# The next head's row of maxima goes into the free columns of the output bank

## The chip, the cores and the metric

The kernel runs on one core of a Trainium2 chip. The metric is device time in microseconds, the median over runs of the same compiled program.

## The reference

A block of three parts on 4 sequences of 1024 tokens of width 128: a mixture-of-experts layer at half weight, attention, and the same expert layer again. Cut to what matters here:

```python
x = x + 0.5 * ffn(layernorm(x))               # 8 experts, 2 chosen for each token
q, k, v = heads(layernorm(x) @ qkv_w + qkv_b)  # 16 heads of width 8, rotary q and k
scores  = einsum('bhqd,bhkd->bhqk', q, k) * 8 ** -0.5
attn    = softmax(scores) @ v                  # 4 x 16 = 64 pairs (b, h), each 1024 x 1024
x = x + attn @ out_w + out_b
x = x + 0.5 * ffn(layernorm(x))
```

The change touches only the attention part, the 64 pairs of sequence and head, called heads 0 to 63 below.

## The kernel before

Each engine has its own instruction stream, written out by hand and kept in step by semaphores. The attention loop handles a head in 16 half steps i = 0 to 15; two of them make one block kb = i // 2 of 128 keys. Four heads make one round of a hardware loop (`Fori`); 14 rounds (heads 4 to 59) run in the loop, the first and the last four heads are written out apart.

**What TensorE does.** In half step i of head n it issues `key_scores` (line 999): 128 keys by 512 queries, transposed scores into one PSUM bank. Beside it, in the other half of the array's rows, it issues `max_scores` (line 966) for head n+2: 128 queries by 512 keys, which serve only to find each query's maximum. After every odd i comes `weigh_values` (line 1014), which multiplies the exponentials of an earlier block (kb - 2) with the values and adds into the head's output bank. Only columns 0 to 255 of the 512 of that bank are used (`QW` = 256). The profile counts each of its four matmuls as two records, x8.

**What the others do.** VectorE reduces each pair of `max_scores` banks, 128 x 1024, to a maximum (line 1262, eight for a head); there are two such pairs of banks, taken in turn, and `max_scores` waits on `max_read` until the pair is free. ScalarE turns each score bank into exponentials (line 750, `probs`, 16 for a head), and copies the finished output of the head before out of PSUM after exponential 3 (line 738, `ot`). GpSimd splits the negated maxima into three bf16 parts (`mparts`).

**The row.** A head's maxima are needed as a row that is part of its query operand. Ahead of `key_scores` of i = 10 (`MT_AT`) of head n, TensorE transposes `mparts` of head n+1 into PSUM (`max_transpose`, line 988). ScalarE copies the result, 24 x 128, to `mrow` (line 730), between exponentials 9 and 10 in its own stream, and a DMA brings it into the operand Q for the next head.

**The ring of banks.** `key_scores` uses three banks in turn. The class `Banks` works out who uses which, and `bank_free` makes a matmul wait until the last user of its bank has been read. The row takes one place in this ring:

```python
if i == MT_AT:
    self.row_user[u] = self.back(user.get(ring[0]), n)
    self.row[u] = ring[0]
    user[ring[0]] = ("row", n, 0)
    ring.append(ring.pop(0))
```

So around the row, before: the transpose waits for exponential 7, key scores 10 for exponential 8, key scores 11 for exponential 9, and key scores 12 for the row's copy. Elsewhere key scores i wait for exponential i - 3 (after the swap of the output bank at i = 6, key scores 6 wait for the copy `ot`). The order of all this is fixed in the code; nothing is planned at run time.

Of the kernel before, what the change touches and what calls it, by code (L numbers as in the profile page):

```python
# [23 lines left out]
BF16 = mybir.dt.bfloat16  # L24
# [4 lines left out]
ACT = mybir.ActivationFunctionType  # L29
AX_X = mybir.AxisListType.X  # L30

P = 128
# [14 lines left out]
NH = B * H  # L47
KB = T // P
PARTS = 3
# [8 lines left out]
QW = T // QUARTERS  # L58
VW = 32
PIECE = H * CH // P  # L60
QSLOTS = 4
# [5 lines left out]
MT_AT = 10  # L67
# [19 lines left out]
class Banks:  # L87


    def __init__(self):  # L90
        self.key, self.row, self.out = ([{} for _ in range(QSLOTS)] for _ in range(3))
        self.key_user, self.row_user, self.out_user = ([{} for _ in range(QSLOTS)] for _ in range(3))
        ring, out = list(SCORE_BANKS), OUT_BANK
        user = {}
        for n in range(2 * QSLOTS):
            u = n % QSLOTS
            for i in range(HALVES):
                if i == OUT_AT:
                    self.out_user[u] = self.back(user.get(ring[0]), n)
                    ring[0], out = out, ring[0]  # L100
                    user[ring[0]] = ("out", n - 1, 0)
                    self.out[u] = out
                if i == MT_AT:
                    self.row_user[u] = self.back(user.get(ring[0]), n)
                    self.row[u] = ring[0]
                    user[ring[0]] = ("row", n, 0)
                    ring.append(ring.pop(0))
                self.key_user[u][i] = self.back(user.get(ring[0]), n)
                self.key[u][i] = ring[0]
                user[ring[0]] = ("key", n, i)  # L110
                ring.append(ring.pop(0))
            if u == QSLOTS - 1:
                assert tuple(ring) == SCORE_BANKS and out == OUT_BANK, (ring, out)
# [6 lines left out]
BANKS = Banks()  # L120
# [35 lines left out]
def build(nc, x_in, qkv_w, qkv_b, v_b, out_w, out_b, wr_t, w1_in, w2_t, cos_t, sin_t, out):  # L156
# [4 lines left out]
    with ExitStack() as ctx:  # L161
# [24 lines left out]
        identb = sb("identb", [P, P], BF16)  # L186
# [49 lines left out]
        mparts = sb("mparts", [P, 2, PARTS, KB], BF16)  # L236
        mrow = sb("mrow", [PARTS * KB, 2, P], BF16)
# [20 lines left out]
        score = [[ps[:, BANKS.key[u][i], :] for i in range(HALVES)] for u in range(QSLOTS)]  # L258
        maxps = [ps[:, MAX_BANK + 2 * s:MAX_BANK + 2 * s + 2, :] for s in range(2)]
        first_maxps = [ps[:, 2 * s:2 * s + 2, :] for s in range(FIRST_PAIRS)]  # L260
        mpsum = [ps[0:PARTS * KB, BANKS.row[u], 0:P // 2].bitcast(BF16) for u in range(QSLOTS)]
        opsum = [ps[:, BANKS.out[u], 0:QW] for u in range(QSLOTS)]


# [49 lines left out]
        mT_in_psum = sem("mT_in_psum")  # L314
# [301 lines left out]
        def _(sc):  # L616
# [106 lines left out]
            def mrow_copy(r, u, beside):  # L723
                n = QSLOTS * r + u
                sc.wait_ge(mT_in_psum, n + 1)

                if not (isinstance(r, int) and r == 0 and u < 2):
                    back = (u - 2) % QSLOTS
                    sc.wait_ge(mrow_loaded[back], 16 * (r + (1 if u >= 2 else 0)))
                nc.scalar.activation(mrow[:, u % 2, :], mpsum[beside], ACT.Copy).then_inc(mrow_ready, 1)  # L730

            def o_copy(r, u):
                n = QSLOTS * r + u
# [26 lines left out]
                    if i == 5 and not more:  # L760
                        xT_copy(NCH, 0, early_t)

            mrow_copy(0, 0, 0)
            for u in range(QSLOTS):
                head(0, u, first=(u == 0))
            with sc.Fori(1, NH // QSLOTS - 1) as r:
# [11 lines left out]
        def _(pe):  # L778
# [192 lines left out]
            def bank_free(n, last):  # L971


                what, dn, i = last
                if what == "key":
                    at_least(pe, probs_ready, HALVES * (n + dn) + i + 1)
                elif what == "row":
                    pe.wait_ge(mrow_ready, n + dn + 2)
                else:
                    at_least(pe, ot_ready, n + dn + 1)  # L980

            def max_transpose(r, u, beside, first=False):

                n = QSLOTS * r + u
                pe.wait_ge(mparts_ready, n + 1)
                if not first:
                    bank_free(n - 1, BANKS.row_user[beside])
                nc.tensor.transpose(mpsum[beside], mparts[:, u % 2, :, :].rearrange("p i t -> p (i t)"),
                                    identb[:]).then_inc(mT_in_psum, 1)

            def key_scores(r, u, i, row):

                n = QSLOTS * r + u
                kb, j = i // 2, i % 2
                if i == 0:
                    pe.wait_ge(mrow_loaded[u], 16 * (r + 1))
                last = BANKS.key_user[u][i]
                bank_free(n, BANKS.row_user[u] if last == ("row", 0, 0) and not row else last)
                nc.tensor.matmul(score[u][i], K[u][0:ROWS, kb * P:(kb + 1) * P],  # L999
                                 Q[u][0:ROWS, j * CH:(j + 1) * CH], start=True, stop=True).then_inc(scores_in_psum, 1)  # L1000

# [19 lines left out]
            pe.wait_ge(head_loaded[1], 32)  # L1021
            for i in range(HALVES):
                if i == FIRST_MT_AT:
                    max_transpose(0, 0, 0, first=True)
                max_scores(0, 1, i)

            pe.wait_ge(v_ready, NCH)
# [2 lines left out]
            def head(r, u, maxes=True, row=True, first=False, early=None, ahead=True):  # L1030
                for i in range(HALVES):
                    kb, j = i // 2, i % 2
                    if i == HALVES - 1 and ahead:
                        operands(r + (u + 3) // QSLOTS, (u + 3) % QSLOTS)
                    if i == MT_AT and row:
                        max_transpose(r + (u + 1) // QSLOTS, (u + 1) % QSLOTS, u)
                    key_scores(r, u, i, row)
                    if maxes:
                        max_scores(r + (u + 2) // QSLOTS, (u + 2) % QSLOTS, i)
                    if j == 1 and kb >= LAG:  # L1040
                        weigh_values(r, u, kb - LAG)
                    elif j == 1 and not first:
                        weigh_values(r + (u - 1) // QSLOTS, (u - 1) % QSLOTS, KB + kb - LAG)
                    if early == 0 and i == 5:

                        pe.wait_ge(max_read, KB * NH)
                        out_projection(0, early_t)
                    if early == 1 and i == 3:
                        x_transposes(NCH, 0, 0, early_t)
                    if early == 1 and i == 9:  # L1050
                        router(NCH, 0, 0, early_r)
# [11 lines left out]
            pe.wait_ge(mrow_ready, NH)  # L1063
            pe.wait_ge(gap_ready, NCH + 1)

            ffn(NCH, True)
# [377 lines left out]
```

## Time and profile before

| | |
|---|---|
| median of 3 runs | 1257.05 us (1257.0 to 1258.89) |
| profiled execution, time | 1257.09 us |
| profiled execution, span | 1255.3 us |
| busy: TensorE, VectorE, ScalarE, GpSimd | 1230.6, 1109.6, 802.1, 149.0 us |
| attention, from the first key scores to the last exponentials | 360 to 955 us |

Busy time is the time in which at least one instruction of the engine is shown as running; instructions overlap, so it says little about slack. The start times of single instructions say more: where the same instruction comes back at a fixed interval with nothing between, the interval is the engine's pace.

### The profile page before, as it was taken

The page shows a single profiled execution, that of the slowest core. Times are in us where ns is not written, and L with a number is a line of the kernel's source. Part 1 is how long each engine was busy: PE and PEld are TensorE (multiplying, and loading weights), DVE is VectorE, ACT ScalarE, POOL GpSimd, SP SyncE. Part 2 cuts the span into 40 slices and gives each one's busy share as a digit, 9 for nine tenths or more (in the row PEclk, how much of TensorE's full clock was granted, in tenths as well). Part 3 has the DMA queues.
Part 4 walks back from the last instruction along what each step waited for, and adds up shares of the span by engine and source line. Part 5 has one row for each costly group of instructions (what it writes and reads, how often), then busy time and mean ns, then how long its engine had stood idle before and what let it go on. Part 6 is the DMA issues. An engine that isn't in the chain of part 4 may idle for free.

```text
span 1255.3 us, 31378 instructions
## 1 busy us (share of the span) xinstructions
PE 1230.6 (98%) x10208; PEld 609.7 (49%) x10208; DVE 1109.6 (88%) x2256; ACT 802.1 (64%) x1546; POOL 149.0 (12%) x454
## 2 busy tenths in 40 slices
PE   6999999999899999999999999999999999999998
PEld 4776666676422222222222222222225777777776
DVE  7889888898789999999999999999995777787775
ACT  5533333333259999999999999999996333333332
POOL 0021222210241111111111111111110000000000
PEclk9999999999869999999999999999999999999999
DMA  7000111002102111111111111111111000000000
GB/s 214 1 26 28 49 51 49 26 29 70 51 21 80 34 42 32 38 36 32 42 32 42 32 32 42 32 42 32 36 47 42 16 18 28 28 28 27 10 9 9
DMA packets 54202, 48.43 MB, mean 39 GB/s; under 512 B 11632, under 2 KB 46960, under 8 KB 54128
## 3 DMA queue, kind: packets, MB, share of 16 engines
q1 hardware_dynamic: 54128, 47.48, 12.4%
q8 instruction: 41, 0.67, 0.2%
q14 instruction: 33, 0.27, 0.1%
HBM read 23.73 MB, written 23.33 MB: 37 GB/s over the span
## 4 chain that ended last, share of the span: by engine, by line
PE 96%; DVE 2%; ACT 1%; issue 0%; DMA 0%; DVEq 0%; ACTq 0%
PE ps L859 26%; PE ps L1014 23%; PE ps L999 22%; PE ps L846 18%; PE ps L814 1%; PE ps L836 1%; PE ps L781 1%; PE ps L966 1%; PE ps L823 1%; PE ps L853 1%; DVE mx L1262 1%; PE ps L873 0%; DVE X L1208 0%; ACT probs L750 0%; DMA X<-x_in 0%
## 5 line engine op out<-in xcount | busy, mean ns | idle before, releaser
L1262 DVE TENSOR_REDUCE mx<-ps 128x1 f32<-128x1024 f32 x512 | 586.0, 1216 | 9.3 <-PE ps L873 4.0
L750 ACT ACTIVATE probs<-ps 128x512 f32<-128x512 f32 x1024 | 551.2, 600 | 32.2 <-PE ps L999 27.7
L669 ACT ACTIVATE sg<-ps,unscale 128x512 f32<-128x512 f32 x256 | 173.6, 687 | 273.9 <-PE ps L859 273.5
L1014 PE MATMUL ps<-probs,vh 128*32 128x256 f32 x4096 | 328.2, 392 | 0.0
L999 PE MATMUL ps<-Q,K 51*128 51x512 bf16 x1024 | 321.6, 384 | 1.8 <-ACT probs L750 0.4
L966 PE MATMUL ps<-K,Q 48*128 48x512 bf16 x1008 | 319.5, 388 | 1.2 <-DVE mx L1262 0.6
L846 PEld LDWEIGHTS ps<-w,act 128*128 128x128 f32 x2048 | 247.9, 192 | 17.8 <-issue 0.8
L846 PE MATMUL ps<-w,act 128*128 128x128 f32 x2048 | 249.3, 275 | 0.0
L1196 DVE SCALAR_TENSOR_TENSOR act<-ps,unscale,sg 128x512 f32<-128x512 f32 x256 | 183.3, 746 | 42.7 <-PE ps L859 17.4
L859 PE MATMUL ps<-x_hi,w_hi 128*128 128x512 f16 x512 | 194.8, 381 | 1.7 <-DVE w_lo L1154 1.0
L859 PE MATMUL ps<-x_lo,w_hi 128*128 128x512 f16 x512 | 194.6, 380 | 0.0
L859 PE MATMUL ps<-x_hi,w_lo 128*128 128x512 f16 x512 | 194.5, 380 | 0.0
L1208 DVE SCALAR_TENSOR_TENSOR X<-ps,rw,X 128x128 f32<-128x128 f32 x512 | 143.9, 344 | 53.8 <-PE ps L846 52.3
L999 PEld LDWEIGHTS ps<-Q,K 51*128 51x128 bf16 x1024 | 75.6, 93 | 227.0 <-ACT probs L750 160.1
L1014 PEld LDWEIGHTS ps<-probs,vh 128*32 128x32 f32 x4096 | 80.9, 108 | 187.6 <-ACT probs L750 146.8
L859 PEld LDWEIGHTS ps<-x_hi,w_lo 128*128 128x128 f16 x512 | 50.2, 98 | 60.9 <-issue 0.8
L966 PEld LDWEIGHTS ps<-K,Q 48*128 48x128 bf16 x1008 | 74.8, 93 | 9.1 <-DVE mx L1262 8.3
L859 PEld LDWEIGHTS ps<-x_hi,w_hi 128*128 128x128 f16 x512 | 51.7, 101 | 53.3 <-issue 3.8
L859 PEld LDWEIGHTS ps<-x_lo,w_hi 128*128 128x128 f16 x512 | 50.2, 98 | 49.8 <-issue 4.9
L559 POOL TENSOR_SCALAR negm<-mx 128x8 f32<-128x8 f32 x64 | 15.1, 236 | 455.6 <-DVE mx L1262 455.6
L517 POOL TENSOR_TENSOR qf<-rot 128x512 f32<-128x512 f32 x14 | 17.8, 1273 | 233.4 <-DVE rot L1243 233.4
L659 ACT ACTIVATE tanh_gap<-gap 128x4 f32<-128x4 f32 x16 | 3.3, 207 | 54.7 <-DVE gap L1165 54.7
(89 smaller groups left out, 605.2 us busy)
## 6 DMA issues: line engine op xcount, KB each, us to landing
o_parts<-ot SPq DMA_DIRECT2D x64, 128.0 KB, 1.9
q_stack<-parts SPq DMA_DIRECT2D x96, 64.0 KB, 2.0
k_stack<-parts SPq DMA_DIRECT2D x96, 64.0 KB, 2.0
Q<-q_stack SPq DMA_DIRECT2D x64, 96.0 KB, 2.3
K<-k_stack SPq DMA_DIRECT2D x64, 96.0 KB, 2.3
probs<-w_in SPq DMA_DIRECT2D x8, 256.0 KB, 5.1
att<-o_parts SPq DMA_DIRECT2D x16, 128.0 KB, 2.6
rden<-rdens SPq DMA_DIRECT2D x16, 128.0 KB, 2.6
```

Of the source, the lines that this page charges most:

```text
L517: nc.gpsimd.tensor_tensor(qf[:, w, :], rot[:, w, 0, :], rot[:, w, 1, :], ALU.add).then_inc(rot_sum, 1)
L559: seq.then(nc.gpsimd.tensor_scalar(negm[:, 0, :], mx[:, s, :], -1.0, None, ALU.mult))
L669: nc.scalar.activation(sg[:, j, :], hid[2 * j], ACT.Silu, scale=unscale[:, e, 2 + j:3 + j]).then_inc(silu_done, 1)
L750: nc.scalar.activation(probs[:, kb % PSLOTS, j * CH:(j + 1) * CH], score[u][i], ACT.Exp, scale=SCALE).then_inc(probs_ready, 1)
L846: last = nc.tensor.matmul(ypsum[s][:, t, :], act[:, s, j, t * P:(t + 1) * P], w2[:, e, j, :], start=(j == 0), stop=(j == 1))
L859: last = nc.tensor.matmul(bank, w[:, e, at:at + P], x[:, k, :], start=(n == 0), stop=(n == 2))
L966: last = nc.tensor.matmul(maxps[t % 2][:, half, :], Q[u][0:STACK, t * P:(t + 1) * P], K[u][0:STACK, half * CH:(half + 1) * CH], start=True ...
L999: nc.tensor.matmul(score[u][i], K[u][0:ROWS, kb * P:(kb + 1) * P], Q[u][0:ROWS, j * CH:(j + 1) * CH], start=True, stop=True).then_inc(scor ...
L1014: last = nc.tensor.matmul(opsum[u][VW * c:VW * (c + 1), :], vh[:, u % 2, kb, :], probs[:, kb % PSLOTS, c * QW:(c + 1) * QW], start=(kb == ...
L1196: nc.vector.scalar_tensor_tensor(out=act[:, e % 2, j, :], in0=hid[2 * j + 1], scalar=unscale[:, e, j:j + 1], in1=sg[:, j, :], op0=ALU.mult ...
L1208: last = nc.vector.scalar_tensor_tensor(out=xt, in0=ypsum[e % 2][:, t, :], scalar=rw[:, k, t, e:e + 1], in1=xt, op0=ALU.mult, op1=ALU.add)
L1262: nc.vector.tensor_reduce(mx[:, u % 2, t:t + 1], pair.rearrange("p a b -> p (a b)"), AX_X, ALU.max).then_inc(max_read, 1)
```

## The change

The transposed row no longer has a place in the ring. It is written into columns 256 to 383 of the output bank of the head that is being worked on, beside the sums that `weigh_values` builds there. Since that bank holds a sum in the making, the row is written by an ordinary matmul with the identity, with `start=False`, and it arrives as fp32, where a transpose left bf16. And since ScalarE must not read a bank that TensorE writes, TensorE now waits for the row's copy (`mrow_ready`) ahead of the next `weigh_values`, behind key scores and max scores 11. The first head's row, ahead of the loop, is transposed as before, into bank 1. ScalarE copies from the new place.

```diff
-                if i == MT_AT:
-                    self.row_user[u] = self.back(user.get(ring[0]), n)
-                    self.row[u] = ring[0]
-                    user[ring[0]] = ("row", n, 0)
-                    ring.append(ring.pop(0))
...
-        mpsum = [ps[0:PARTS * KB, BANKS.row[u], 0:P // 2].bitcast(BF16) for u in range(QSLOTS)]
+        mpsum = [ps[0:PARTS * KB, BANKS.out[u], QW:QW + P] for u in range(QSLOTS)]
+        first_mpsum = ps[0:PARTS * KB, 1, 0:P // 2].bitcast(BF16)
...
-            def max_transpose(r, u, beside, first=False):
+            def max_transpose(r, u, beside):
                 n = QSLOTS * r + u
                 pe.wait_ge(mparts_ready, n + 1)
-                if not first:
-                    bank_free(n - 1, BANKS.row_user[beside])
-                nc.tensor.transpose(mpsum[beside], mparts[:, u % 2, :, :].rearrange("p i t -> p (i t)"),
-                                    identb[:]).then_inc(mT_in_psum, 1)
+                rows = mparts[:, u % 2, :, :].rearrange("p i t -> p (i t)")
+                if beside is None:
+                    nc.tensor.transpose(first_mpsum, rows, identb[:]).then_inc(mT_in_psum, 1)
+                else:
+                    nc.tensor.matmul(mpsum[beside], rows, identb[:], start=False, stop=True, skip_group_check=True).then_inc(mT_in_psum, 1)
...
                     if maxes:
                         max_scores(r + (u + 2) // QSLOTS, (u + 2) % QSLOTS, i)
+                    if i == MT_AT + 1 and row:
+                        pe.wait_ge(mrow_ready, QSLOTS * r + u + 2)
                     if j == 1 and kb >= LAG:
                         weigh_values(r, u, kb - LAG)
```

TensorE's stream in the loop around the row, in a head of the first place of a round, before: from the weighing ahead of the row to key scores 12.

```order
L1014 MATMUL ps<-probs,vh 32x256 x3
L84 REGISTER_ALU [waits mparts_ready]
L988 MATMUL ps<-identb,mparts 24x128 [waits probs_ready]
L84 REGISTER_ALU
L999 MATMUL ps<-Q,K 128x512 [waits probs_ready]
L965 REGISTER_ALU
L966 MATMUL ps<-K,Q 128x512 [waits max_read]
L84 REGISTER_ALU
L999 MATMUL ps<-Q,K 128x512 [waits probs_ready]
L966 MATMUL ps<-K,Q 128x512
L1014 MATMUL ps<-probs,vh 32x256 [waits probs_ready]
L999 MATMUL ps<-Q,K 128x512 [waits mrow_ready]
```

The same place in the changed kernel (line 985 is the row, 994 the key scores, 962 the max scores, 1009 the weighing):

```order
L1009 MATMUL ps<-probs,vh 32x256 x3
L985 MATMUL ps<-identb,mparts 24x128 [waits mparts_ready]
L84 REGISTER_ALU
L994 MATMUL ps<-Q,K 128x512 [waits probs_ready]
L961 REGISTER_ALU
L962 MATMUL ps<-K,Q 128x512 [waits max_read]
L84 REGISTER_ALU
L994 MATMUL ps<-Q,K 128x512 [waits probs_ready]
L962 MATMUL ps<-K,Q 128x512
L1009 MATMUL ps<-probs,vh 32x256 [waits probs_ready,mrow_ready]
L84 REGISTER_ALU
L994 MATMUL ps<-Q,K 128x512 [waits probs_ready]
```

The row has lost its wait for an exponential, the wait for the row's copy has moved from key scores 12 up to the weighing in front of them, and the waits of key scores 10, 11 and 12 are now for exponentials 7, 8 and 9, one earlier than before for the first two. ScalarE's stream has the same instructions in the same order as before; here its piece around the row in the changed kernel, for the second place of a round (line 746 are the exponentials, 726 is the row's copy):

```order
L84 REGISTER_ALU [waits scores_in_psum]
L746 ACTIVATE probs<-ps 128x512 [waits probs_used]
L742 REGISTER_ALU
L746 ACTIVATE probs<-ps 128x512 [waits scores_in_psum]
L721 REGISTER_ALU
L725 REGISTER_ALU [waits mT_in_psum]
L726 ACTIVATE mrow<-ps 24x128 [waits mrow_loaded3]
L742 REGISTER_ALU
L84 REGISTER_ALU [waits scores_in_psum]
L746 ACTIVATE probs<-ps 128x512 [waits probs_used]
```

The row's copy still stands behind exponentials 8 and 9 and ahead of exponential 10.

## Rows read from the trace of the kernel before

**Rows 1.** The page: TensorE's busy time, and the chain that ended last by engine.

```profile
PE 1230.6 (98%) x10208; PEld 609.7 (49%) x10208; DVE 1109.6 (88%) x2256; ACT 802.1 (64%) x1546; POOL 149.0 (12%) x454
...
PE 96%; DVE 2%; ACT 1%; issue 0%; DMA 0%; DVEq 0%; ACTq 0%
```

**Rows 2.** One round of four heads: stretch, its length, busy time by engine, clock.

```profile
451.75:488.52 36.77, 36.68 (x392) 10.65 (x388) 36.58 (x33) 35.33 (x73) 5.01 (x24) 1.00 0.12 36
```

**Rows 3.** Timeline of TensorE around a row: start, length, what.

```profile
707.56 0.64 PE L1014 MATMUL ps<-probs,vh 128*32 128x256 f32 x8
708.13 0.39 PE L999 MATMUL ps<-Q,K 51*128 51x512 bf16 x1
...
708.36 0.38 PE L999 MATMUL ps<-Q,K 51*128 51x512 bf16 x1
...
708.66 0.64 PE L1014 MATMUL ps<-probs,vh 128*32 128x256 f32 x8
709.12 0.22 PE L988 MATMUL ps<-identb,mparts 128*24 128x128 bf16 x1
709.28 0.39 PE L999 MATMUL ps<-Q,K 51*128 51x512 bf16 x1
...
709.77 0.39 PE L999 MATMUL ps<-Q,K 51*128 51x512 bf16 x1
...
710.09 0.64 PE L1014 MATMUL ps<-probs,vh 128*32 128x256 f32 x8
710.66 0.39 PE L999 MATMUL ps<-Q,K 51*128 51x512 bf16 x1
```

**Rows 4.** Timeline of ScalarE there: exponentials 7 and 8, 8, 9, the copy.

```profile
708.02 1.21 ACT L750 ACTIVATE probs<-ps 128x512 f32<-128x512 f32 x2
...
708.63 0.60 ACT L750 ACTIVATE probs<-ps 128x512 f32<-128x512 f32 x1
...
709.12 0.59 ACT L750 ACTIVATE probs<-ps 128x512 f32<-128x512 f32 x1
709.60 0.25 ACT L730 ACTIVATE mrow<-ps 24x128 bf16<-24x128 bf16 x1
```

**Rows 5.** Timeline of VectorE in several stretches: start, length of a merged run, count.

```profile
705.59 1.22 DVE L1262 TENSOR_REDUCE mx<-ps 128x1 f32<-128x1024 f32 x1
...
705.59 4.61 DVE L1262 TENSOR_REDUCE mx<-ps 128x1 f32<-128x1024 f32 x4
...
708.98 2.47 DVE L1262 TENSOR_REDUCE mx<-ps 128x1 f32<-128x1024 f32 x2
...
699.74 2.55 DVE L1262 TENSOR_REDUCE mx<-ps 128x1 f32<-128x1024 f32 x2
...
924.18 10.27 DVE L1262 TENSOR_REDUCE mx<-ps 128x1 f32<-128x1024 f32 x9
```

**Rows 6.** The row's transposes from 441 to 893 us: durations, first and last start.

```profile
L988 PE MATMUL ps<-identb,mparts x50: 219/219/219, 442.6 to 893.0; 128*24 128x128 bf16 x50
```

**Rows 7.** ScalarE's two kinds of copies: shortest, median, longest ns, first and last start.

```profile
L730 ACT ACTIVATE mrow<-ps x64: 252/253/267, 353.5 to 940.4; 24x128 bf16<-24x128 bf16 x64
L738 ACT ACTIVATE ot<-ps x64: 384/390/427, 375.6 to 955.9; 128x256 f32<-128x256 f32 x64
```

**Rows 8.** Timeline at a row whose copy found ScalarE idle.

```profile
369.02 0.31 PE L988 MATMUL ps<-identb,mparts 128*24 128x128 bf16 x1
...
369.37 0.27 ACT L730 ACTIVATE mrow<-ps 24x128 bf16<-24x128 bf16 x1 [0.44 <-PE ps L988]
```

**Rows 9.** Timeline of TensorE at a row ahead of the hardware loop.

```profile
387.55 0.22 PE L988 MATMUL ps<-identb,mparts 128*24 128x128 bf16 x1
...
388.44 0.42 PE L1014 MATMUL ps<-probs,vh 128*32 128x256 f32 x4
```

**Rows 10.** The last max scores on TensorE; all maxima, with the last start.

```profile
932.65 0.38 PE L966 MATMUL ps<-K,Q 48*128 48x512 bf16 x1
...
L1262 DVE TENSOR_REDUCE mx<-ps x512: 1160/1215/1226, 329.2 to 933.2; 128x1 f32<-128x1024 f32 x171
```

More of the change, by code:

```diff
@@ L90, in __init__ @@
     def __init__(self):
-        self.key, self.row, self.out = ([{} for _ in range(QSLOTS)] for _ in range(3))
-        self.key_user, self.row_user, self.out_user = ([{} for _ in range(QSLOTS)] for _ in range(3))
+        self.key, self.out = ([{} for _ in range(QSLOTS)] for _ in range(2))
+        self.key_user, self.out_user = ([{} for _ in range(QSLOTS)] for _ in range(2))
         ring, out = list(SCORE_BANKS), OUT_BANK
@@ L729, in mrow_copy @@
                     sc.wait_ge(mrow_loaded[back], 16 * (r + (1 if u >= 2 else 0)))
-                nc.scalar.activation(mrow[:, u % 2, :], mpsum[beside], ACT.Copy).then_inc(mrow_ready, 1)
+                nc.scalar.activation(mrow[:, u % 2, :], first_mpsum if beside is None else mpsum[beside], ACT.Copy).then_inc(mrow_ready, 1)
             def o_copy(r, u):
@@ L761, in head @@
                         xT_copy(NCH, 0, early_t)
-            mrow_copy(0, 0, 0)
+            mrow_copy(0, 0, None)
             for u in range(QSLOTS):
@@ L976, in bank_free, with key_scores @@
                     at_least(pe, probs_ready, HALVES * (n + dn) + i + 1)
-                elif what == "row":
-                    pe.wait_ge(mrow_ready, n + dn + 2)
                 else:
                     at_least(pe, ot_ready, n + dn + 1)
-            def max_transpose(r, u, beside, first=False):
+            def max_transpose(r, u, beside):
                 n = QSLOTS * r + u
                 pe.wait_ge(mparts_ready, n + 1)
-                if not first:
-                    bank_free(n - 1, BANKS.row_user[beside])
-                nc.tensor.transpose(mpsum[beside], mparts[:, u % 2, :, :].rearrange("p i t -> p (i t)"),
-                                    identb[:]).then_inc(mT_in_psum, 1)
-            def key_scores(r, u, i, row):
+                rows = mparts[:, u % 2, :, :].rearrange("p i t -> p (i t)")
[3 more added lines that the diff above has]
+                    nc.tensor.matmul(mpsum[beside], rows, identb[:], start=False, stop=True, skip_group_check=True).then_inc(mT_in_psum, 1)
+            def key_scores(r, u, i):
                 n = QSLOTS * r + u
@@ L996, in key_scores @@
                     pe.wait_ge(mrow_loaded[u], 16 * (r + 1))
-                last = BANKS.key_user[u][i]
-                bank_free(n, BANKS.row_user[u] if last == ("row", 0, 0) and not row else last)
+                bank_free(n, BANKS.key_user[u][i])
                 nc.tensor.matmul(score[u][i], K[u][0:ROWS, kb * P:(kb + 1) * P],
@@ L1023, in _ @@
                 if i == FIRST_MT_AT:
-                    max_transpose(0, 0, 0, first=True)
+                    max_transpose(0, 0, None)
                 max_scores(0, 1, i)
@@ L1036, in head @@
                         max_transpose(r + (u + 1) // QSLOTS, (u + 1) % QSLOTS, u)
-                    key_scores(r, u, i, row)
+                    key_scores(r, u, i)
                     if maxes:
                         max_scores(r + (u + 2) // QSLOTS, (u + 2) % QSLOTS, i)
+                    if i == MT_AT + 1 and row:
+                        pe.wait_ge(mrow_ready, QSLOTS * r + u + 2)
                     if j == 1 and kb >= LAG:
@@ L1062, in _ @@
             pe.wait_ge(ot_ready, NH)
-            pe.wait_ge(mrow_ready, NH)
             pe.wait_ge(gap_ready, NCH + 1)
```

## Prediction

> **What bounds the kernel now.** I read the page first. The chain that ended last is TensorE in 96%, and TensorE is busy 98% of the span [rows 1]. That doesn't tell what a change in attention is worth, since VectorE is nearly as full there: in one round of four heads, 36.77 us long, TensorE is busy for 36.68 us, VectorE for 36.58 and ScalarE for 35.33, at full clock [rows 2]. Three engines look saturated, so shares decide nothing, and I went to start times.
>
> TensorE's timeline shows the weighings (line 1014) at 707.56 and 708.66, 1.107 us apart in finer figures, and the next at 710.09, 1.43 later [rows 3]. So seven blocks of a head take TensorE 1.107 us each, and the block with the row takes 1.427: 7 x 1.107 + 1.427 = 9.176 us a head. The extra 0.32 us isn't the transpose itself. Key scores 10 start 0.16 after the transpose, but key scores 11 come 0.49 after those [rows 3], where two neighbours elsewhere in a head are 0.23 apart (708.13 and 708.36). ScalarE's rows say why: exponential 9 starts at 709.12 and lasts 0.59, so it ends at 709.71, and key scores 11 start 0.06 later [rows 3, 4]. Exponential 8 ends at 709.23, and key scores 10 start 0.05 behind it. The ring has lost a bank to the row, so TensorE waits for two exponentials that elsewhere it wouldn't need.
>
> VectorE follows. One maximum shows 1.22 us, four in a row 4.61, so they start (4.61 - 1.22) / 3 = 1.13 us apart [rows 5]. The longest undisturbed run, nine in 10.27 us, gives 1.131 [rows 5]. This is VectorE's pace with nothing to wait for: 8 x 1.131 = 9.05 us a head. At the row two maxima take 2.47 instead of 2.35 us, and in the head that stands two places behind the start of a loop round 2.55 [rows 5]. So VectorE idles 0.12 us a head in three heads and 0.20 in the fourth, 0.14 on average. It agrees with the transposes: 50 of them between 442.6 and 893.0, so 49 heads of 9.19 us [rows 6]; 9.19 - 9.05 = 0.14.
>
> TensorE sets the pace by 0.14 us a head, and right below it lies VectorE's floor of 9.05 us. This is the figure that limits any gain here.
>
> **The change part by part.** *The ring place.* Key scores 10 and 11 now wait for exponentials 7 and 8, each one exponential (0.49 us, 708.63 to 709.12 [rows 4]) earlier. Both are done when TensorE comes there: key scores 10 may start 0.15 after the row, key scores 11 0.23 later, so 0.38 behind the row where now it is 0.65. By this alone the weighing could follow 0.31 later at 0.69, instead of 0.97 [rows 3].
>
> *The new wait.* The weighing must now wait for the row's copy. The copy stands behind exponential 9 on ScalarE and starts 0.48 behind the row (709.12 to 709.60 [rows 3, 4]); it lasts 0.25, and 0.06 is the delay from an end on ScalarE to a start on TensorE measured above. So the weighing starts 0.48 + 0.25 + 0.06 = 0.79 behind the row: 0.10 is idle time of a new kind, and of 0.28 won 0.18 is left. Behind the waiting instruction stand key scores 12 and max scores 12, so ScalarE and VectorE would both feel a longer wait; VectorE works on an earlier pair then. The block with the row becomes 0.46 (708.66 to 709.12) + 0.79 = 1.25 us, and TensorE's head 7 x 1.107 + 1.25 = 9.00, with the 0.02 that a loop round adds on average 9.02. That is below VectorE's 9.05, so VectorE becomes the bound, by a hair.
>
> *What the row costs.* The trace has no identity matmul of this shape that isn't a transpose. From below it is the 0.219 us of the transpose [rows 6], from above the 0.39 of a 512-column matmul [rows 3]; I take 0.22, since columns and operands are the same. At 0.39 key scores 11 and the weighing would come 0.17 later, at 0.86 behind the row, and the head would be 9.09: saving 0.10 instead of 0.14. The copy isn't hurt as much: with ScalarE idle it started 0.35 behind the row [rows 8], now it starts at 0.48 because exponential 9 is ahead of it. The Trainium skill's page "Perfetto Trace Analysis" says under "Transposes" that a logical transpose should use the transpose and not a standard matmul, which speaks against this part. By that rule the row gets dearer; the sum by it would be the 9.09 just given.
>
> *The copy.* It now reads fp32. From below it is 0.25 us as now, from above the 0.39 of the copy of 128 x 256 fp32 [rows 7]; I take 0.25, since there are still 128 elements a partition. At 0.39 the weighing starts at 0.93, the head is 9.16, and 0.03 a head is saved.
>
> *Nothing else.* The DMA that follows the copy has the rest of the head, over 6 us, and its place in the queue stays. The first head's row keeps its form. What is moved in the register work is a single instruction from in front of the row to behind the weighing, under its 0.57 us (710.09 to 710.66 [rows 3]).
>
> *The sum.* VectorE's idle time at the row goes away in the heads whose maxima lie beside loop heads 4 to 59: 56 x 0.14 = 7.9 us. The heads ahead of the loop have a shorter stall (the weighing 0.89 behind the row [rows 9], so 0.08 less, hence 0.04 above VectorE's floor instead of 0.12); three of them and the restart give 0.2. Head 62 has no maxima any more and TensorE runs alone, so its row saves the full 0.18. Last, a bound VectorE lets TensorE run ahead as far as the two pairs of banks allow: the pair's second matmul would start 2 x 1.131 - 1.22 - 0.06 - 0.23 = 0.76 ahead of its maximum, where the last one now starts 0.58 ahead (932.65 to 933.2 [rows 10]): 0.2 more for what follows. Together 7.9 + 0.2 + 0.2 + 0.2 = 8.5 us. The profiled execution took 1257.09 us, of it 1255.3 span, and is equal to the median of 1257.05: 1257.1 - 8.5 = 1248.6 us.
>
> **The rivals.** A measurement of this kernel can tell about 0.2%, 2.5 us, from no change.
>
> *TensorE stays the bound.* VectorE's floor is only 0.03 above TensorE's new pace, so anything that lengthens the wait for the copy by more is paid in full. For it: neither the fp32 copy nor the matmul is in the trace, and a restart behind a wait at the weighing isn't either. Against: both have the same element count. With the dear matmul the time is 56 x 0.10 + 0.4 = 6.0 less, 1251.1; with the dear copy 56 x 0.03 + 0.4 = 2.1 less, 1255.0.
>
> *No change.* The copy stands behind the same exponential 9 that holds key scores 11 now. If the wait for it cost 0.18 us more than I count (dear copy and a little more), one stall would have replaced the other: 1257.
>
> *Slower.* The new wait puts TensorE at the mercy of ScalarE's queue. If ScalarE reaches exponential 9 later, by more than the 0.18 us that is left, each further 0.1 costs 56 x 0.1 = 5.6 us, since VectorE and ScalarE both wait behind the weighing. The place is the backlog that the copy `ot` (0.39 us behind exponential 3 [rows 7]) makes: a backlog of 0.3 that still stood at exponential 8 would give 56 x 0.12 = 6.7 us more, 1263.8. Against: exponential 8 starts 0.61 behind exponential 7 (708.02 to 708.63), where full pace is 0.49, so ScalarE has caught up by then, with 0.12 to spare [rows 4], and blocks get no shorter. "Perfetto Trace Analysis" has under "Matmuls" the rule that independent matmul groups should rotate through different banks, so that evacuation overlaps the next group. The change goes against that, and by the rule the evacuation lies bare; what of it lies bare here by rows is the 0.10 us above.
>
> **How the numbers follow.** VectorE's floor, 1248.6: 0.74, its own range 1247.9 to 1249.7. TensorE still the bound, 1250 to 1255: 0.14. No change: 0.07. Slower: 0.05. The range from 1247.7 to 1253.0 holds the first and two thirds of the second, some 0.83. Of the second a small part lies within 0.2% of before, so faster 0.87, same 0.08, slower 0.05.
>
> **What would show it.** Maxima 1.131 us apart through the row, without the 2.47 and 2.55; the rows' matmuls 9.05 us apart in every head; key scores 11 about 0.4 behind the row and the weighing 0.6 to 0.8 behind it; `max_scores` waiting for VectorE in ordinary blocks, which TensorE's timeline doesn't show now. I am wrong if the weighing starts more than 0.85 behind the row, if the copy takes over 0.3 us, or if maxima slow down once they run without a pause.

## The result, and the profile after

The changed kernel takes 1248.37 us (median of 4 runs: 1250.74, 1247.19, 1249.06, 1247.67), the kernel before 1257.88 us in its 4 runs beside it (1257.0 to 1258.89). The ratio is 0.9929, with a 95% interval of 0.9917 to 0.9942: faster by 0.7%. Forecast were 1248.6 us, from 1247.7 to 1253.0. The profiled execution of the changed kernel is the slowest of its four, 1250.74 us, and that needs an explanation of its own, below. Two of its four times lie under the lower end of the range.

Line numbers of the changed kernel: the row is line 985, key scores 994, max scores 962, the weighing 1009, the row's copy 726, the exponentials 746, VectorE's maxima 1259.

The profile's page of the changed kernel, the lines that answer to [rows 1]: busy time by engine, then the chain that ended last by engine and by line.

```profile
PE 1224.7 (98%) x10208; PEld 617.9 (49%) x10208; DVE 1104.0 (88%) x2256; ACT 803.0 (64%) x1546; POOL 149.0 (12%) x454
...
PE 53%; DVE 35%; issue 10%; ACT 0%; DMA 0%; DVEq 0%; ACTq 0%
DVE mx L1259 34%; PE ps L855 27%; PE ps L842 18%; PE ps L1009 2%; PE ps L994 1%; PE ps L810 1%; PE ps L832 1%; PE ps L777 1%; PE ps L819 1%; PE ps L849 1%; PE ps L869 0%; PE ps L962 0%; DVE X L1205 0%; ACT probs L746 0%; PE ps L795 0%
```

Busy time tells as little as before: TensorE is still at 98%. The chain tells it: it was TensorE for 96%, and now VectorE's maxima hold 34% of it, and most of the 10% "issue" are the 0.2 to 0.3 us between one maximum and the next. In attention the bound has passed from TensorE to VectorE.

VectorE's timeline in the changed kernel: start, length of a run, count.

```profile
698.71 1.21 DVE L1259 TENSOR_REDUCE mx<-ps 128x1 f32<-128x1024 f32 x1
...
698.71 9.13 DVE L1259 TENSOR_REDUCE mx<-ps 128x1 f32<-128x1024 f32 x8
...
599.16 101.89 DVE L1259 TENSOR_REDUCE mx<-ps 128x1 f32<-128x1024 f32 x90
```

In the stretch up to 701 us ninety maxima run without a pause, eleven heads long: (101.89 - 1.21) / 89 = 1.131 us apart. The runs of [rows 5] with 2.47 and 2.55 us for two maxima are gone.

The rows' matmuls in the changed kernel, from 440 to 880 us (answers to [rows 6]), and the copies of the whole kernel (answers to [rows 7]): shortest, median and longest ns, first and last start.

```profile
L985 PE MATMUL ps<-identb,mparts x49: 219/219/219, 440.8 to 875.2; 128*24 128x128 bf16 x49
...
L726 ACT ACTIVATE mrow<-ps x64: 252/253/267, 353.2 to 931.3; 24x128 bf16<-24x128 f32 x63, 24x128 bf16<-24x128 bf16 x1
```

(875.2 - 440.8) / 48 = 9.05 us a head, where it was 9.19. The matmul with the identity takes 219 ns like the transpose before, and the copy out of fp32 253 ns like the copy out of bf16.

TensorE's timeline around a row in the changed kernel (answers to [rows 3]).

```profile
702.77 0.64 PE L1009 MATMUL ps<-probs,vh 128*32 128x256 f32 x8
703.23 0.22 PE L985 MATMUL ps<-identb,mparts 128*24 128x128 bf16 x1
703.38 0.39 PE L994 MATMUL ps<-Q,K 51*128 51x512 bf16 x1
...
703.60 0.38 PE L994 MATMUL ps<-Q,K 51*128 51x512 bf16 x1
...
703.99 0.64 PE L1009 MATMUL ps<-probs,vh 128*32 128x256 f32 x8
704.56 0.39 PE L994 MATMUL ps<-Q,K 51*128 51x512 bf16 x1
```

Key scores 11 start 0.38 behind the row, where it was 0.65, and the weighing 0.76, where it was 0.97. The block with the row takes 703.99 - 702.77 = 1.22 us instead of 1.43.

The same timeline at an ordinary block, and the same stretch of ScalarE with the row's copy (answers to [rows 4]).

```profile
699.95 0.39 PE L994 MATMUL ps<-Q,K 51*128 51x512 bf16 x1
699.98 0.39 PE L962 MATMUL ps<-K,Q 48*128 48x512 bf16 x1
```

```profile
703.68 0.25 ACT L726 ACTIVATE mrow<-ps 24x128 bf16<-24x128 f32 x1
```

In an ordinary block the max scores now start 0.03 behind the key scores: they wait for VectorE to give their banks back. (With shorter maxima, in e6 below, both start at 601.84 again.) At the row the two start together (703.38 both in the full timeline), since there TensorE is late and the banks are free. The copy starts 0.45 behind the row and ends at 703.93, 0.06 ahead of the weighing: what the weighing waits for is the copy.

**Where the 6.4 us of the span came from.** VectorE's last maximum starts at 924.3 instead of 933.2 [rows 10], 8.9 us earlier. Of these, 0.3 lie ahead of the first key scores, 0.7 in the heads ahead of the loop, 7.8 in the loop and 0.1 at its exit. After the last maximum 2.5 us are given back. These are the windows from the last maximum to the first matmul of the last expert layer, first of the changed kernel (with the stretch of 6.8 us inside it), then of the kernel before: stretch, length, busy time of TensorE, its weight loads, VectorE, ScalarE and GpSimd, then the granted clock, DMA share and GB/s.

```profile
924.30:949.90 25.60, 24.67 (x201) 7.77 (x197) 11.07 (x52) 19.64 (x42) 1.75 (x6) 0.87 0.04 12
930.00:940.00 10.00, 9.80 (x86) 2.67 (x86) 4.83 (x27) 9.55 (x20) 0.00 (x0) 1.00 0.05 15
942.00:948.80 6.80, 6.80 (x44) 1.73 (x47) 2.25 (x20) 3.35 (x7) 0.00 (x0) 0.50 0.00 0
```

```profile
933.30:956.30 23.00, 22.03 (x205) 7.30 (x197) 10.99 (x52) 19.78 (x42) 1.76 (x6) 1.00 0.04 13
```

In the changed kernel's profiled execution the granted clock falls to one half (1.2 GHz) from 942.0 to 948.8, in head 63. TensorE's timeline there shows two key scores in 1.03 us and a weighing of 1.08 us, where at full clock the weighing lasts 0.64:

```profile
943.11 1.08 PE L1009 MATMUL ps<-probs,vh 128*32 128x256 f32 x8
944.12 1.03 PE L994 MATMUL ps<-Q,K 51*128 51x512 bf16 x2
945.08 1.08 PE L1009 MATMUL ps<-probs,vh 128*32 128x256 f32 x8
```

Up to there TensorE was hardly idle: from 930 to 940 it was busy for 9.80 of 10 us. One gap follows, of 0.44 us, in which key scores wait for an exponential, and then the eight matmuls of the next expert layer's router, which have only 8 columns each. These stand in the changed kernel's timeline right ahead of the fall:

```profile
940.24 0.39 PE L994 MATMUL ps<-Q,K 51*128 51x512 bf16 x1 [0.44 <-ACT probs L746]
...
941.12 1.09 PE L832 MATMUL ps<-wr,xnT 128*128 128x8 f32 x8
```

The change added no work in heads 62 and 63. Whether this fall belongs to the change at all is asked by the runs from e8 on.

### The profile page after: what moved, and what is told of

The parts are those of the page before. It is cut to its first block, busy times and chain, and to the rows that moved or that the text cites. A ratio compares the mean times of both kernels' runs of the same rounds, so it can differ in the third digit from the quotient of the medians.

```text
span 1248.9 us, 31420 instructions
## 1 busy us (share of the span) xinstructions
PE 1224.7 (98%) x10208; PEld 617.9 (49%) x10208; DVE 1104.0 (88%) x2256; ACT 803.0 (64%) x1546; POOL 149.0 (12%) x454
## 4 chain that ended last, share of the span: by engine, by line
PE 53%; DVE 35%; issue 10%; ACT 0%; DMA 0%; DVEq 0%; ACTq 0%
DVE mx L1259 34%; PE ps L855 27%; PE ps L842 18%; PE ps L1009 2%; PE ps L994 1%; PE ps L810 1%; PE ps L832 1%; PE ps L777 1%; PE ps L819 1%; PE ps L849 1%; PE ps L869 0%; PE ps L962 0%; DVE X L1205 0%; ACT probs L746 0%; PE ps L795 0%
## 5 line engine op out<-in xcount | busy, mean ns | idle before, releaser
L994 PE MATMUL ps<-Q,K 51*128 51x512 bf16 x1024 | 312.1, 385 | 0.4 <-ACT probs L746 0.4
L962 PE MATMUL ps<-K,Q 48*128 48x512 bf16 x1008 | 309.0, 387 | 1.4 <-DVE mx L1259 0.6
L994 PEld LDWEIGHTS ps<-Q,K 51*128 51x128 bf16 x1024 | 83.2, 93 | 206.4 <-ACT probs L746 167.0
L962 PEld LDWEIGHTS ps<-K,Q 48*128 48x128 bf16 x1008 | 82.7, 93 | 9.4 <-DVE mx L1259 8.6
```

## The experiments

**My theory:** the gain is the ring place. Key scores 10 and 11 no longer wait for exponentials 8 and 9, TensorE's head falls below VectorE's floor of 9.05 us, and VectorE takes over. **The rivals:** the matmul with the identity or the new wait has a part in it, as a gain or a cost that another part hides; TensorE, not VectorE, is still the bound; and the wait for the copy can turn the gain into a loss if the copy comes more than 0.18 us later.

### The two other parts of the change alone

The wait alone, in the kernel before (e1_wait_only):

```diff
                         max_scores(r + (u + 2) // QSLOTS, (u + 2) % QSLOTS, i)
+                    if i == MT_AT + 1 and row:
+                        pe.wait_ge(mrow_ready, QSLOTS * r + u + 2)
                     if j == 1 and kb >= LAG:
```

> The kernel before, row still in the ring, with one thing added: TensorE also waits for the row's copy ahead of the weighing that follows key scores 11. Theory (the stall is the ring's wait for exponentials 8 and 9, and the new wait ends sooner than it): the copy's wait would end 0.79 us behind the row, the weighing starts 0.97 behind it anyway, so heads stay at 9.19 us on average and the time at 1257, within 1.5 us. Rival (the new wait costs TensorE something wherever it stands, as an extra instruction and a restart): 0.05 us or more a head, 1260 or more.

The matmul alone, into the ring bank that the transpose had (e2_matmul_in_ring):

```diff
-        mpsum = [ps[0:PARTS * KB, BANKS.row[u], 0:P // 2].bitcast(BF16) for u in range(QSLOTS)]
+        mpsum = [ps[0:PARTS * KB, BANKS.row[u], 0:P] for u in range(QSLOTS)]
...
-                nc.tensor.transpose(mpsum[beside], mparts[:, u % 2, :, :].rearrange("p i t -> p (i t)"),
-                                    identb[:]).then_inc(mT_in_psum, 1)
+                nc.tensor.matmul(mpsum[beside], mparts[:, u % 2, :, :].rearrange("p i t -> p (i t)"),
+                                 identb[:], start=True, stop=True).then_inc(mT_in_psum, 1)
```

> The kernel before with only the form of the row changed: a matmul with the identity into the ring bank in place of the transpose, fp32, copied from fp32. Theory: the form brings nothing and costs nothing; the row shows 0.22 us and the copy 0.25, the heads stay at 9.19, the time at 1257 within 1.5 us. Rival (part of the gain comes from the form): 1255 or less. Rival (an ordinary matmul is dearer than a transpose): key scores 10 move from 0.16 behind the row to up to 0.33; since exponential 9 holds key scores 11 the time may hide that, so the rows decide.

Measured: ratios to the kernel before of 1.0003 (0.999 to 1.0015) and 1.0003 (0.9993 to 1.0012). In both, the head stays at 9.192 us and the weighing 0.97 behind the row. These are the rows' matmuls and the copies of e2 over the whole kernel.

```profile
L988 PE MATMUL ps<-identb,mparts x64: 218/219/280, 352.9 to 938.8; 128*24 128x128 bf16 x64
...
L730 ACT ACTIVATE mrow<-ps x64: 254/254/266, 353.2 to 939.2; 24x128 bf16<-24x128 f32 x64
```

219 and 254 ns, against 219 and 253 of the bf16 forms [rows 6, 7]. Neither part brings or costs anything by itself, so what the whole change brings is the ring place (with the output bank as the place that makes it free). This is by elimination: no run frees the ring place alone, since the row must go somewhere. The wait alone costs nothing here because exponential 9 holds the same block for longer: in e1 the copy ends 0.24 us ahead of the weighing.

### The wait for the copy made longer

The changed kernel with one (e3_two_copies) or two (e4_three_copies) useless copies of the row ahead of the real one on ScalarE:

```diff
+                nc.scalar.activation(spare[:], first_mpsum if beside is None else mpsum[beside], ACT.Copy)
                 nc.scalar.activation(mrow[:, u % 2, :], first_mpsum if beside is None else mpsum[beside], ACT.Copy).then_inc(mrow_ready, 1)
```

> The changed kernel with a second, useless copy of the row ahead of the real one on ScalarE, which makes the copy end about 0.18 us later. Theory (TensorE's pace lies 0.03 to 0.04 us a head below VectorE's floor and the wait for the copy is on it): the weighing starts about 0.95 behind the row, the heads go from 9.05 to about 9.18, and the time rises by 57 x 0.13 = 7 us to about 1255. Rival (VectorE bounds and hides ScalarE's delay): under 2 us more, about 1249.

> The changed kernel with two useless copies of the row ahead of the real one. Theory: another 0.18 us on each head, all of it paid: heads of 9.36 us, some 17 to 18 us above the changed kernel, 1266, which is slower than the kernel before; this is the slower rival of the prediction made to happen. Rival (the delay is hidden behind VectorE): under 1252.

Measured against the kernel before: e3 0.9995 (0.9982 to 1.0008), e4 1.008 (1.006 to 1.01). Timelines of a row in e3 and in e4: start, length, what.

```profile
615.38 0.22 PE L987 MATMUL ps<-identb,mparts 128*24 128x128 bf16 x1
...
615.86 0.25 ACT L727 ACTIVATE spare<-ps 24x128 bf16<-24x128 f32 x1
616.02 0.26 ACT L728 ACTIVATE mrow<-ps 24x128 bf16<-24x128 f32 x1
...
616.33 0.42 PE L1011 MATMUL ps<-probs,vh 128*32 128x256 f32 x4 [0.19 <-ACT mrow L728]
```

```profile
610.95 0.22 PE L988 MATMUL ps<-identb,mparts 128*24 128x128 bf16 x1
...
611.74 0.26 ACT L729 ACTIVATE mrow<-ps 24x128 bf16<-24x128 f32 x1
...
612.06 0.62 PE L1012 MATMUL ps<-probs,vh 128*32 128x256 f32 x5 [0.35 <-ACT mrow L729]
```

The weighing now starts 0.95 and 1.11 behind the row, each time 0.06 behind the end of the real copy, and the heads take 9.168 and 9.328 us. Both are somewhat below what I had expected (9.18 and 9.36), since small copies stand 0.16 apart on ScalarE and not 0.18. With the weighing at 0.763 the head was 9.050: 0.18 more of wait cost 0.12, and the next 0.16 cost 0.16 in full. The kink is what two nearly equal bounds look like. So the wait for the copy is on TensorE's path, it has about 0.06 us of cover by VectorE, and the slower rival is real: at 0.34 us more it takes the whole gain and 0.8% with it.

The forecast time of e3, 1255 us, came in its profiled execution (1254.8) and three more of its ten (1254.82 to 1255.62); the other six lie from 1258.31 to 1259.63, so its median missed by 3.5 us. Its profile has no half clock at the end; the split of the times into groups comes up again below.

The Trainium skill's page "Perfetto Trace Analysis" asks under "Matmuls" that independent matmul groups rotate through different banks. In these runs what the breach of it costs follows how late the copy ends: in e3, e4 and e6 (below) TensorE's head is 8.22 us plus the distance of the weighing from the row, each time.

### How far TensorE lies below VectorE's floor

VectorE made faster in both kernels: its maxima read 768 of 1024 columns, with everything else as it is (e5_before_short_max, e6_after_short_max):

```diff
+SEEN = 3 * 2 * 512 // 4
...
-                nc.vector.tensor_reduce(mx[:, u % 2, t:t + 1], pair.rearrange("p a b -> p (a b)"), AX_X,
+                nc.vector.tensor_reduce(mx[:, u % 2, t:t + 1], pair.rearrange("p a b -> p (a b)")[:, 0:SEEN], AX_X,
```

> The kernel before, with VectorE's maxima over 768 of the 1024 columns of each pair (so the row of maxima leaves out a quarter of the keys). One maximum takes about 0.87 us in place of 1.13. Theory (TensorE set the pace before, through its stall at the row): the heads in the loop stay at 9.19 us; only the first two heads and the first eight maxima, which VectorE bounds, get shorter, by 2 to 5 us in all. Rival (VectorE was already a bound together with TensorE): the heads get shorter, toward 9.0 or less, and the time falls by 10 us or more.

> The changed kernel with the same shorter maxima (a quarter of the keys left out of the row). Theory: VectorE no longer bounds and TensorE's own pace shows: 9.00 us a head, 9.02 with the loop's share, so only 0.03 to 0.04 us a head less than the 9.05 of the changed kernel, about 2 us in all beside the 2 to 5 us of the start that the kernel before gains too. Rival (TensorE could have gone much faster): heads of 8.9 us or less, 8 us or more on top.

Measured against the kernel before: e5 0.9982 (0.9969 to 0.9995), e6 0.9902 (0.9877 to 0.9927). VectorE's timeline of e5:

```profile
598.72 0.96 DVE L1263 TENSOR_REDUCE mx<-ps 128x1 f32<-128x768 f32 x1
599.82 6.49 DVE L1263 TENSOR_REDUCE mx<-ps 128x1 f32<-128x768 f32 x6
606.78 0.96 DVE L1263 TENSOR_REDUCE mx<-ps 128x1 f32<-128x768 f32 x1 [0.47 <-PE ps L967]
```

A maximum lasts 0.96 instead of 1.22 us, but six of them stand (6.49 - 0.96) / 5 = 1.106 us apart, which is TensorE's pace, and at the row VectorE idles 0.47 us for the max scores. The heads of the loop stay at 9.19: a faster VectorE changes nothing there, so TensorE was the bound. Of the 0.2%, 1.1 us lie ahead of the loop, where the maxima of head 1 take 8.41 instead of 9.48 us. TensorE's timeline at a row in e6, from the block ahead of it:

```profile
601.84 0.38 PE L995 MATMUL ps<-Q,K 51*128 51x512 bf16 x1
601.84 0.38 PE L963 MATMUL ps<-K,Q 48*128 48x512 bf16 x1
602.14 0.64 PE L1010 MATMUL ps<-probs,vh 128*32 128x256 f32 x8
602.60 0.22 PE L986 MATMUL ps<-identb,mparts 128*24 128x128 bf16 x1
...
602.98 0.38 PE L995 MATMUL ps<-Q,K 51*128 51x512 bf16 x1
...
603.39 0.42 PE L1010 MATMUL ps<-probs,vh 128*32 128x256 f32 x4
```

With VectorE out of the way the weighing is 0.79 behind the row, the block with the row lasts 1.25 us, and the head takes 9.008. That is TensorE's own head in the changed kernel. It lies 0.04 below VectorE's 9.050: VectorE is the bound, by a hair. The weighing stands 0.41 behind the second key scores (603.39 - 602.98) where in the block before it is 0.30 (602.14 - 601.84): 0.11 us is what the wait for the copy costs TensorE. One of e6's times is 1243.21 us, the other three lie from 1247.32 to 1247.51, and the profiled one of these has the half clock at the end.

### No row at all

In the changed kernel, from head 4 on, neither matmul, copy nor DMA of the row (e7_no_row):

```diff
             def head(r, u, maxes=True, row=True, first=False, early=None, ahead=True):
+                row = row and isinstance(r, int) and r == 0 and u < 3
```

with the matching conditions at ScalarE's copy and SyncE's DMA, and key scores and GpSimd that no longer wait for it. The operands keep the rows of heads 0 to 3.

> The changed kernel with the row left out from head 4 on: no transpose, no copy, no DMA of the row, the operands keep the rows of heads 0 to 3. Theory: VectorE's floor holds the heads at 9.05 us, the same as with the row, though TensorE alone would need 8 x 1.107 = 8.86; the time is that of the changed kernel less at most 1 us (head 62 has no maxima to hold it). Rival (the row still costs something on the bound): up to 0.19 us a head less, 1240 or below.

Measured: 0.993 (0.9906 to 0.9954), 1248.86 us, the same as the changed kernel within the interval. VectorE's timeline of e7:

```profile
599.62 100.77 DVE L1261 TENSOR_REDUCE mx<-ps 128x1 f32<-128x1024 f32 x89
```

(100.77 - 1.21) / 88 = 1.131 us. Without the row the head is the same 9.05 us: the change has taken all that was to be had at this place, and what is left of the row costs nothing while VectorE is the bound.

### The fall of the clock at the end

The half clock of 6.8 us in head 63 stands in the profiles of e1, e2, e4, e5 and e6 as well, and not in those of the kernel before, e3 and e7. So it comes with and without the change. What sets heads 62 and 63 apart from the loop is that no max scores run beside the key scores: TensorE is busy by time, but the key scores use 51 of the 128 rows with nothing beside them. To test that, e8_after_filled_tail puts a useless matmul of the max scores' shape beside each key score there; e9_after_again is the changed kernel once more, e10_filled_tail_again is e8 once more.

```diff
+            def filler(u, i):
+                s, t, half = (u + 2) % QSLOTS, i // 2, i % 2
+                if u == 2 and i == 0:
+                    pe.wait_ge(max_read, KB * NH - 1)
+                nc.tensor.matmul(ps[:, MAX_BANK, :], Q[s][0:STACK, t * P:(t + 1) * P],
+                                 K[s][0:STACK, half * CH:(half + 1) * CH], start=True, stop=True)
...
                     if maxes:
                         max_scores(r + (u + 2) // QSLOTS, (u + 2) % QSLOTS, i)
+                    else:
+                        filler(u, i)
```

> The changed kernel with useless matmuls, shaped like max scores, beside each key score of heads 62 and 63, which have no max scores of their own, into a bank that is free there. In the profiled execution of the changed kernel TensorE's clock fell to half for 6.8 us from about 942 us, inside head 63, and the stretch from the last maximum to the first matmul of the last part took 25.6 us where the kernel before took 23.1. Theory (the clock falls there because TensorE does less in these two heads): the clock stays at full in that stretch, 22.7 to 23.1 us of it, and the runs come together near 1247.5 instead of 1247.2 to 1250.7. Rival (the fall has another cause, or depends on chance only): it still shows in some executions and the runs scatter as before.

> The changed kernel once more, beside the next three on one chip. The profiles so far show TensorE's clock at half for 27.3, 30.7 or 34.1 us from about 336 us, and for 6.8 us or not at all in head 63 (half in it in six of ten profiles); by rows these cost about 1.0 to 1.9 us and 2.9 us. Theory: with heads of 9.05 us in every execution, the time falls into groups between 1247 and 1251, median 1247.5 to 1250.

> The changed kernel with the useless matmuls in heads 62 and 63 once more. Theory (the fall in head 63 comes from too little work on TensorE there): no half clock in the profile between 900 and 1200 us, and no time in the highest group: all within 1247.0 to 1249.6. Rival (chance): the half clock shows again, or single times near 1251.

Measured: e8 0.9921 (0.9901 to 0.994), e9 0.993 (0.9915 to 0.9945), e10 0.9923 (0.991 to 0.9936). Windows from the last maximum to the first matmul of the last expert layer, for e8, e9 and e10:

```profile
925.80:948.60 22.80, 21.86 (x234) 7.32 (x230) 11.09 (x52) 19.68 (x42) 1.75 (x6) 1.00 0.04 13
```

```profile
925.40:950.80 25.40, 24.46 (x204) 7.72 (x197) 11.10 (x52) 19.69 (x42) 1.75 (x6) 0.87 0.04 12
```

```profile
924.60:947.40 22.80, 21.86 (x234) 7.35 (x231) 11.04 (x52) 19.69 (x41) 1.75 (x6) 1.00 0.04 13
```

With more matmuls (x234 instead of x204) the stretch is 2.6 us shorter, and the clock stays up. What e8 expected of the times, that they come together near 1247.5, didn't come: they lie from 1247.21 to 1249.38.

The filling isn't the only thing that sets the place apart. In each of the eight profiles with the fall, it comes 0.7 to 2.1 us behind the start of the router's eight matmuls in head 63. But the same gap and the same eight matmuls stand in all 14 profiles, and so in the ones where the clock stays up; here is e12, which has the filled tail:

```profile
940.06 0.39 PE L1001 MATMUL ps<-Q,K 51*128 51x512 bf16 x1 [0.43 <-ACT probs L746]
...
940.95 1.06 PE L832 MATMUL ps<-wr,xnT 128*128 128x8 f32 x8
```

No run moves or leaves out the router's matmuls, so their part in the fall isn't tested.

A second place where a half clock stands is the start of attention, from 336 us on for 27 to 34 us. e11_filled_start puts 12 useless matmuls beside the max scores of head 1, e12_filled_both has both fillings.

```diff
+                if i < HALVES - 4:
+                    nc.tensor.matmul(ps[:, 2, :], w1_hi[HALF:HALF + STACK, 0, 0:P], x_hi[HALF:HALF + STACK, 0, :],
+                                     start=True, stop=True)
                 max_scores(0, 1, i)
```

> The changed kernel with twelve useless matmuls beside the max scores of head 1 (about 351 to 358 us), in the other half of the rows, where TensorE otherwise waits for VectorE at half clock. Theory (the half clock of about 31 us from 336 us lasts as long as TensorE has little to do, and slows heads 0 and 1): it ends about 7 us earlier, the maxima of head 2, which took 11.2 to 12.5 us, take under 10.5, and the time falls by 1 to 3 us. Rival: the clock comes back at the same time as before, no gain.

> The changed kernel with both fillings, start and tail. Theory: the two gains add: no half clock in the tail, a shorter one at the start, times of 1244.5 to 1248 with less scatter, and the fastest of all versions by its median. Rival: no better than the better one of the two alone.

Measured: e11 0.9928 (0.9915 to 0.9941), e12 0.992 (0.9908 to 0.9933), 1247.64 us. Windows of e11 at the start:

```profile
335.50:352.60 17.10, 13.08 (x34) 4.90 (x34) 11.63 (x29) 5.33 (x8) 5.13 (x9) 0.50 0.02 8
352.60:356.00 3.40, 2.17 (x16) 0.52 (x14) 3.40 (x4) 1.55 (x2) 3.32 (x4) 1.00 0.13 35
356.00:369.70 13.70, 12.98 (x60) 2.31 (x56) 11.58 (x10) 6.75 (x14) 4.82 (x11) 0.50 0.03 7
```

In e11 the clock came back for 3.4 us only. In that stretch TensorE was busy for 2.17 of 3.40 us, and the clock fell again. The maxima of head 2 took 11.74 us, where under 10.5 were expected. The theory that this filling would end the slow stretch falls; it ends no sooner than without, and no time is gained. In e12, with the same filling, the clock didn't come back at all for 30.7 us from 337.0 on, though TensorE was busy for 3.32 of the 3.40 us from 352.6 to 356.0. So the short return can't be put down to the filling, and e12's median, which lies in the range expected of it, holds no gain at the start. The tail, again, has no half clock:

```profile
924.10:946.90 22.80, 21.86 (x234) 7.35 (x231) 11.05 (x52) 19.68 (x41) 1.75 (x6) 1.00 0.04 12
```

**What the times say with it.** The changed kernel with an unfilled tail (its own runs, e9 and e11, 16 times) has 7 times from 1250.39 to 1251.6, 8 from 1247.14 to 1247.67, and one at 1249.06. With the filled tail (e8, e10, e12, 14 times) none lies above 1249.4. The 3 profiles of the former have the half clock in head 63, the 3 of the latter don't. With a fall in 8 of 11 unfilled profiles, three without one could come by luck; 0 of 14 times against 7 of 16 say more (on the chip of e9 to e12, 0 of 10 against 6 of 12). The upper group disappears, but the medians, 1247.6 to 1248.9 against 1248.4 to 1249.4, aren't told apart by their intervals. The best version measured is e12 at 0.992, and it isn't shown to beat the plain change at 0.993. Nor is it shown what in the filling counts, the filled rows or just more matmuls.

## Why the prediction was right

- **What bounded the kernel before.** TensorE's 9.19 us above VectorE's floor of 9.05: e5 shows the first (a faster VectorE changes no head of the loop), e7 and the run of 90 maxima the second (9.05 with and without the row).
- **The ring place.** Key scores 11 were to start 0.38 behind the row, and start 0.378 behind it. That the gain is this part and no other follows from e1 and e2, where the other two do nothing alone.
- **The new wait.** The weighing at 0.79 behind the row by the sum; 0.763 measured, and 0.787 in e6. That it waits for the copy is shown by e3 and e4, which move it one for one. The waits on TensorE from 450 to 850 us put a number on the idle time of a new kind, below: engine, what it waited for, us in total, times, longest.

```profile
PEld ps L1009 <- ACT mrow L726: 19.9, 45, 0.5
```

  These 45 waits, 0.44 us each, are counted from the end of the last weight load and so hold more than matmul idle time; the loss to the path was put at 0.10 us (0.79 against 0.69), and e6's rows show 0.11. No run has the changed kernel without the wait, so 0.69 itself isn't measured.
- **The row's matmul and its copy.** 0.22 and 0.25 us forecast, 0.219 and 0.253 measured. Of the two bounds the lower one held for both. The rule of the Trainium skill's page "Perfetto Trace Analysis" under "Transposes", that a standard matmul should not stand in for the transpose, finds nothing to warn of in this shape: e2 exchanges one for the other at 219 ns each.
- **The block and TensorE's head.** 1.25 and 9.02 us forecast; 1.22 measured beside the bound VectorE, 1.25 and 9.01 in e6, where TensorE runs by its own pace.
- **The loop.** 56 x 0.14 = 7.9 us forecast, 7.8 measured, or 7.9 with the 0.1 at the exit. This is the main term, and its mechanism is the one that was forecast.
- **The small terms, mis-sized.** The heads ahead of the loop gave 0.7 instead of 0.2 us. Some 0.4 of it is head 2, whose maxima took 11.23 instead of 11.66 us in a stretch where the clock is half at first; in e8 the same head took 12.47, so this is scatter of the clock and no gain to count on. For the tail, its last row and TensorE's lead, 0.4 were forecast; at full clock it is 22.8 us (e8, e10, e12, though with the filling in it) against 23.0 to 23.1 before, which is 0.2 to 0.3. TensorE's lead for it was worked out as 0.76 us; the terms given add up to 0.75, which changes nothing.
- **What the sum didn't have, and luck.** The half clock in head 63 costs 2.6 to 3.0 us (25.4 to 25.6 us of tail against 22.8 in the changed kernel, 26.0 in e1 and e2 against 23.1 before) and came in 7 of 16 executions, by the times. It isn't part of the change: the kernel before scatters too, 24 of its 53 times on record lie from 1256.37 to 1257.39 us and the others from 1258.7 up. The sum started from an execution in the lower group (1257.09). The lower group of the changed kernel lies at 1247.14 to 1247.67, which is 9.7 us below that of the kernel before, by their medians, and under the forecast range; 8.5 were forecast. That the median of 1248.37 comes within 0.3 us of 1248.6 is luck: it lies between the two groups of times. The two profiles account for 9.2 us with the tail at full clock (8.9 and 0.3), of which 0.7 is scatter (0.3 ahead of attention, 0.4 in head 2); without that it is the forecast 8.5. What makes up the rest to 9.7 isn't known.

What stays open: why the clock falls in some executions and not in others with the same instructions, whether the router's matmuls in head 63 have a part in it, and what would keep it up at the start of attention.

## What to carry to other kernels

When several engines look full, take each one's pace in a head (the interval of its back-to-back instructions) and look for the block that breaks it: here one of eight blocks was 0.32 us too long, and the worth of any cure was capped at 0.14 by the next engine's floor. A buffer that is used once a head but takes a place in a ring costs the users behind it a step of slack, here key scores 10 and 11; columns that lie free in a bank with another rhythm cost none, provided that what empties them ends before the next writer needs the bank, and an extra copy in that chain, which delays it by 0.16 to 0.18 us, is enough to lose nearly all of the gain (heads of 9.168 against 9.192). Two engines 0.04 us apart in 9.05 are one bound: less work for TensorE alone brought nothing (e7), less for VectorE alone 0.04 us a head (e6).

## What was unexpected of the hardware

- **The clock can fall with TensorE busy.** In head 63 it was granted one half for 6.8 us, at 2.6 to 3.0 us of cost. In the changed kernel TensorE had been busy for 9.80 us from 930 to 940, and then idle once for 0.44 us ahead of the fall at 942.0. With the same key scores and weighings and useless matmuls in the other half of the rows, it stayed up in 3 profiles of 3; unfilled, it fell in 8 of 11. TensorE's busy time alone doesn't tell the two apart: the same gap, 0.43 us, stands in the filled e12.
- **Added work can cost less than nothing.** 32 useless matmuls beside the key scores left the stretch 2.6 to 2.8 us shorter than the unfilled one at half clock, and within 0.3 us of the unfilled one at full clock (22.8 against 23.0).
- **The same filling, two outcomes.** In e11 the clock came back for 3.4 us, in which TensorE was busy for 2.17, and fell again; in e12 the same stretch, busy for 3.32 of 3.40 us, stayed at one half throughout.
- **Small copies.** On ScalarE copies of 24 x 128 last 0.25 us each but stand 0.16 us apart, so each further one delays what waits by 0.16 and not by 0.25.
